# A three-layer transformer on one core: the norm in three slots, its modulation applied per channel after the transposition

## What is computed

```python
mod = silu(c) @ w_adaln + b_adaln                  # 6 vectors of 144 channels per sample
sh_msa, sc_msa, g_msa, sh_mlp, sc_mlp, g_mlp = split(mod, 6)
h = ln(x) * (1 + sc_msa) + sh_msa                  # ln: (x - mean) * rsqrt(var + eps), per token
x = x + g_msa * attention(h @ w_qkv + b_qkv) @ w_proj
h = ln(x) * (1 + sc_mlp) + sh_mlp
x = x + g_mlp * mlp(h)                             # layer 0: 4 experts, top 2; gelu
...
x = x + ((x @ U) @ expm(A(c)) - x @ U) @ U.T       # U = qr(P), after the three layers
```

## Time and profile before

| | us |
|---|---|
| median of 3 runs | 911.35 (909.35 to 921.39) |
| the profiled execution, its own time | 919.2 |
| its span, first to last instruction | 917.2 |
| TensorE matmuls busy in it | 751.5 |
| VectorE busy | 556.0 |
| ScalarE busy | 386.0 |
| GpSimd busy | 181.0 |
| mean granted TensorE clock (1.00 is full) | 0.856 |

### The profile page before, as it was taken

The page is one execution under the profiler, slowest core; times in us unless marked ns, Lnnn a source line. Parts: engine busy times, 40 slices in busy tenths (PEclk is TensorE's granted clock), DMA queues, the critical chain, the costliest instruction groups (busy, mean ns, idle before and its releaser), DMA issues.

```text
span 917.2 us, 11092 instructions
## 1 busy us (share of the span) xinstructions
PE 751.5 (82%) x3571; PEld 438.5 (48%) x3571; DVE 556.0 (61%) x1614; ACT 386.0 (42%) x690; POOL 181.0 (20%) x372
## 2 busy tenths in 40 slices
PE   6597889967998799798867886979897789979746
PEld 1353444335764445366444343645443555436325
DVE  3477787886327558752465777474787666785242
ACT  0221465534444544254235442435453356646511
POOL 5502012440132300302323003021003110021020
PEclk9955899989997669799977997976897988999957
DMA  3210100110121000012100000100000101000000
GB/s 88 69 35 7 32 14 22 39 31 13 48 56 32 1 24 13 12 33 60 39 18 1 24 12 13 32 1 1 24 13 11 33 1 25 12 12 1 13 1 13
DMA packets 22714, 21.23 MB, mean 23 GB/s; under 512 B 4831, under 2 KB 17015, under 8 KB 22658
## 3 DMA queue, kind: packets, MB, share of 16 engines
q1 hardware_dynamic: 22610, 20.52, 8.6%
q10 hardware_dynamic: 48, 0.02, 0.0%
HBM read 13.62 MB, written 0.61 MB: 16 GB/s over the span
## 4 chain that ended last, share of the span: by engine, by line
PE 62%; DVE 28%; issue 4%; ACT 2%; POOL 2%; DMA 0%; DVEq 0%; SPq 0%; ACTq 0%; POOLq 0%
PE m_bank L1400 11%; PE o_bank L1422 10%; DVE row_max L972 9%; PE s_bank L1383 8%; PE d_bank L1539 7%; PE d_bank L1483 3%; PE m_bank L1592 3%; PE m_bank L1409 2%; DVE h_tok L1031 2%; PE d_bank L1528 2%; PE d_bank L1440 2%; PE d_bank L1439 1%; PE d_bank L1454 1%; PE d_bank L1530 1%; PE d_bank L1529 1%
## 5 line engine op out<-in xcount | busy, mean ns | idle before, releaser
L797 ACT ACTIVATE probs<-s_bank 128x512 f32<-128x512 f32 x384 | 223.1, 598 | 380.4 <-PE s_bank L1383 377.1
L972 DVE TENSOR_REDUCE row_max<-m_bank 128x1 fp32r<-128x512 f32 x384 | 255.3, 686 | 91.8 <-PE m_bank L1400 86.5
L1400 PE MATMUL m_bank<-k_pad,q_t 128*128 128x512 f32 x348 | 173.1, 511 | 43.0 <-DVE row_max L972 12.6
L1383 PE MATMUL s_bank<-q_t,k_pad 128*128 128x512 f32 x384 | 176.3, 466 | 2.9 <-ACT probs L797 2.0
L1400 PEld LDWEIGHTS m_bank<-k_pad,q_t 128*128 128x128 f32 x348 | 72.1, 212 | 115.0 <-issue 36.8
L1422 PE MATMUL o_bank<-probs,v_aug 128*32 128x512 f32 x768 | 120.6, 704 | 0.7 <-ACT probs L797 0.7
L1383 PEld LDWEIGHTS s_bank<-q_t,k_pad 128*128 128x128 f32 x384 | 81.8, 215 | 30.1 <-ACT probs L797 15.4
L1539 PE MATMUL d_bank<-w,g_act 128*128 128x144 f32 (+1 forms) x480 | 61.8, 288 | 8.7 <-issue 8.7
L1539 PEld LDWEIGHTS d_bank<-w,g_act 128*128 128x128 f32 (+1 forms) x480 | 59.5, 190 | 14.2 <-issue 8.3
L714 POOL TENSOR_TENSOR h_tok<-h_tok,mod 128x144 f32<-128x144 f32 x48 | 23.7, 494 | 202.7 <-DVE h_tok L1031 202.7
L1592 PE MATMUL m_bank<-gram_rows,ident 64*64 64x208 f32 (+42 forms) x128 | 40.3, 403 | 16.0 <-DVE gram_rows L1207 15.6
(11 more groups left out here) (232 smaller groups left out, 1145.1 us busy)
## 6 DMA issues: line engine op xcount, KB each, us to landing
k_pad<-k_t SPq DMA_DIRECT2D x96, 64.0 KB, 2.0
raw_a<-in_L_cond_w_dram SPq DMA_DIRECT2D x10, 288.0 KB
w<-in_L_cond_w_dram SPq DMA_DIRECT2D x10, 288.0 KB
w_rows<-in_L_cond_W_dram SPq DMA_DIRECT2D x8, 141.8 KB
raw_d<-in_L_cond_w_dram SPq DMA_DIRECT2D x30, 36.0 KB
x_tok<-in_x_dram SPq DMA_DIRECT2D x2, 288.0 KB, 4.5
w<-in_L_cond_W_fc_dram SPq DMA_DIRECT2D x2, 288.0 KB
raw_a<-in_L_cond_W_fc_dram SPq DMA_DIRECT2D x2, 288.0 KB
```

What stands on the lines that cost most here:

```text
L797: act.activation(probs[:, n % PROBS, :], s_banks[n % S_BANKS][:, :], ACT.Exp, scale=HD ** -0.5)\
L972: dve.tensor_reduce(row_max[:, grp % 2, t, MAXROW + 32 * j:MAXROW + 32 * j + 1], bk[:, :], AX.X, ALU.max).then_inc(drained, 1)
L1383: pe.matmul(s_banks[n % S_BANKS][:, :], k_pad[:, grp % PADS, j, kt * P:(kt + 1) * P], q_t[:, par, g, :], start=True, stop=True).then_inc(s ...
L1400: ins = pe.matmul(bk[:, :], q_t[:, par, g, t * P:(t + 1) * P], k_pad[:, grp % PADS, j, :], start=True, stop=True)
```

## The change

- The norm of kinds "msa" and "mlp" has five slots, room 2, 1, 2, 1, 2: VectorE does the statistics in the first, the reciprocal root in the second, the scaling in the third, each with a fill ahead of it or in it; TensorE turns in the fourth and fifth; the hi, lo and d parts are made in the fifth. Kinds "o" and "x" become a stage `lay` of three slots, room 2, 1, 2.
- The modulation is no longer applied to tokens. `mods(l)` computes shift and 1 + scale per channel on partitions (`mod_a`, `mod_d`) by matmuls of two columns; `gates(l)` computes the two gates as before, for tokens. After the transposition ScalarE writes `h_hi` and `h_d` with scale and bias; VectorE computes `h_part` (rows 32 to 64) and `h_full`, and `h_lo` from `h_full` and `h_hi`; GpSimd subtracts for rows 32 to 64 of `h_d`.
- GpSimd only copies the last 16 channels. `x_tok` and `o_tok` rows are as wide as those of `h_tok`, so "o" and "x" are turned where they lie.
- Slots: `mods(0)` alone stands in HEAD, `gates(0)` in block 0, `mods(1)` and `mods(2)` in blocks 1 and 3, `gates(1)` in 2, `gates(2)` in 4. `load_ada(1)` leaves the start of SyncE's queue. GpSimd has a dozen more small constants.

```diff
-HEAD = [("mods", 0, 0), ("mods", 0, 1), ("prep", 0), ("norm", 0, "msa"), ("qkv", 0)]
+HEAD = [("mods", 0), ("prep", 0), ("norm", 0, "msa"), ("qkv", 0)]
...
-ROOM = {"prep": (), "mods": (1,), "norm": (4, 1, 2), ...
+ROOM = {"prep": (), "mods": (1,), "gates": (1,), "norm": (2, 1, 2, 1, 2), "lay": (2, 1, 2), ...
...
# GpSimd, norm
-                    if kind in ("msa", "mlp"):
-                        link(pool.tensor_tensor(tile, tile, mv[:, first + 1, :], ALU.mult))
-                        link(pool.tensor_tensor(tile, tile, mv[:, first, :], ALU.add))
-                    elif kind == "o":
-                        link(pool.tensor_copy(tile, o_tok[:, blk % 2, t, :]))
...
+                    pool.wait_ge(s["h_part_ready"], seen.next("modulated"))
+                    pool.wait_ge(s["h_d_ready"], seen.n["norm"])
+                    pool.tensor_tensor(h_d[32:64, :], h_part[32:64, :], h_d[32:64, :].bitcast(F32), ALU.subtract)\
+                        .then_inc(d_free, 1)
...
# ScalarE, norm, last slot
+                act.activation(h_hi[:, :], a_bank[:, :], ACT.Identity, scale=scale, bias=shift)\
+                    .then_inc(s["h_hi_ready"], 1)
+                act.wait_ge(s["h_part_ready"], seen.next("modulated"))
+                act.activation(h_d[:, :], d_bank[0:DW, :], ACT.Identity, scale=mod_d[:, l % 2, v + 1, b:b + 1],
+                               bias=mod_d[:, l % 2, v, b:b + 1]).then_inc(s["h_d_ready"], 1)
...
# VectorE, norm
+                    yield
+                    fill[0]()
                     link(dve.tensor_scalar(nwt[:, 1, 0:T], mean_var[:, :, 1], EPS, None, ALU.add))
                     rsqrt(rstd[:, :], nwt[:, 1, 0:T], nwt[:, 0, 0:T])
+                    yield
+                    fill[0]()
...
+                    dve.tensor_scalar(h_part[32:64, :], d_bank[32:64, :], mod_d[32:64, l % 2, v + 1, b:b + 1],
+                                      mod_d[32:64, l % 2, v, b:b + 1], ALU.mult, ALU.add)\
+                        .then_inc(s["h_part_ready"], 1)
+                    dve.wait_ge(s["h_hi_ready"], seen.n["norm"])
+                    link(dve.tensor_scalar(h_full[:, :], a_bank[:, :], mod_a[:, l % 2, v + 1, b:b + 1],
+                                           mod_a[:, l % 2, v, b:b + 1], ALU.mult, ALU.add))
+                    dve.tensor_tensor(h_lo[:, :], h_full[:, :], h_hi[:, :].bitcast(F32), ALU.subtract)\
+                        .then_inc(a_free, 1)
...
# TensorE, mods
+                for i, v in enumerate((0, 1, 3, 4)):
+                    for ada, c, first in ((ada_a, c_wide_a, True), (ada_d, c_wide_d, False)):
+                        pe.matmul(bk[:, B * i:B * (i + 1)], ada[:, v * C:v * C + P], c[:, :, 0], start=first,
+                                  stop=not first)
+                    for ada, c, first in ((ada_a, c_wide_a, True), (ada_d, c_wide_d, False)):
+                        for r in range(0, DW, 32):
+                            ins = pe.matmul(bk[r:r + 32, B * (4 + i):B * (5 + i)], ada[:, v * C + P:v * C + P + 32],
+                                            c[:, :, 0], start=first, stop=not first, skip_group_check=True)
```

More of the change, by code:

```diff
@@ L88, in stages @@
     if block == 0:
-        out += [("norm", 1, "msa"), ("qkv", 1), ("prep", 1), ("prep", 2), ("mods", 1, 0), ("prep", 3)]
+        out += [("norm", 1, "msa"), ("qkv", 1), ("gates", 0), ("prep", 1), ("prep", 2), ("prep", 3)]
     if block >= 1:
@@ L279, in load_order @@
     todo += [(mlp_at_step(m - 2) + 1 if m >= 2 else -1, ("w2", m)) for m in range(1, MLPS)]
-    todo += [(LAST_SLOT[("mods", 1, 1)], ("ada", 2))]
+    todo += [(LAST_SLOT[("gates", l - 1)], ("ada", l)) for l in range(1, LAYERS)]
     todo += [(-0.5, ("pad", grp)) for grp in range(PADS)]
@@ L343, in build @@
         h_d = sb("h_d", [DW, N], F32R)
+        h_part = sb("h_part", [DW, N])
+        h_full = sb("h_full", [P, N])
         ada_a = sb("ada_a", [P, 6 * C])
@@ L580, in _ @@
             load_w(1)
-            load_ada(1)
             load_item(1)
@@ L720, in norm @@
-                yield
-                ring.take(), ring.take()
-                yield
+                for t in range(T):
+                    if kind == "x":
+                        pool.wait_ge(s["x_done"], blk % B * 2 + t // 2 + 1)
+                    elif kind != "o":
+                        pool.wait_ge(s["xn_ready"], seen.next("xn_ready"))
+                    tile = token_tile(blk, kind, t)
+                    pool.tensor_copy(tile[:, P + 32:P + DW].rearrange("p (r w) -> p r w", r=2)[:, :, 0:CR],
+                                     tile[:, P:C].unsqueeze(1).to_broadcast([P, 2, CR]))\
+                        .then_inc(s["h_tok_ready"], 1)
+                    pool.wait_ge(s["h_tok_ready"], seen.next("h_tok_ready"))
@@ L802, in o_copy, with mods @@
                 act.activation(o_t[:, :], o_bank[:, :], ACT.Copy).then_inc(s["o_copied"], 1)
-            def norm(blk, kind):
+            mods_done = {}
+            def mods(l):
+                _, drained, before = ring.take()
+                mods_done[l] = (drained, before + 1)
+                yield
+            def norm(blk, kind):
+                b, l = blk % B, blk // B
+                v = 0 if kind == "msa" else 2
+                if kind in ("msa", "mlp"):
+                    yield
+                    yield
                 yield
@@ L1444, in norm @@
             def norm(blk, kind):
+                if not h_ready:
+                    pe.wait_ge(s["ident_ready"], 1)
+                if kind in ("msa", "mlp"):
+                    yield
+                    yield
                 yield
@@ L1644, in solver @@
                 last[chain] = ready
-            walk = {"mods": mods, "norm": norm, "qkv": qkv, "proj": proj, "gate": gate, "mlp": mlp,
-                    "rotate": rotate}
+            walk = {"mods": mods, "gates": gates, "norm": norm, "lay": norm, "qkv": qkv, "proj": proj, "gate": gate,
+                    "mlp": mlp, "rotate": rotate}
             def side(todo):
```

229 lines of the change are left out of this document (135 added, 94 removed).

## The result

The changed kernel took 955.53 us in the median of four runs (948.87 to 960.12), against 914.28 for the kernel before beside it (909.35 to 921.39). The ratio is 1.044, with a 95% interval of 1.034 to 1.054: it is slower, where I had said 877 us and a range that ended at 914. The profiled execution took 948.87 us. Some executions of either kernel are disturbed, at a lower clock and some per cent longer: a ratio leaves them out, a median holds them.

The account below looks back on a forecast made before the run. It took the kernel to be bound by TensorE and VectorE waiting for each other, chiefly at the norms, neither being full. Its terms summed to -34.3 us, from 911.35 to 877 us, with an 8-in-10 range of 849 to 914.

Parts of the forecast that it names:

- (h): Small things: earlier turning of "o" in blocks 1 and 2, loss 2 us; SyncE's loads and the rest hidden.
- (d): Clock behind the ten norms between steps: less time at half speed, gain 16 us, ends 0 and 32.
- Rival 2: Closings between steps: ScalarE held by VectorE, exponentials late, TensorE stands; slower, 944 us; chance 0.06.
- (a): HEAD's modulation: two-column matmul passes replace sixteen passes of 432 columns, gain 4.8 us.
- Rival 4: Modulation matmuls in HEAD and between steps: loads of 32 columns nearly free, 0.03 us each; 869 us; chance 0.11.
- (b): HEAD's norm: GpSimd's multiplication and addition go, transpositions end sooner, closing loses 0.9; gain 1.1 us in all.
- (c): Stalls at the ten norms between steps: VectorE's work in three parts frees TensorE, gain 20 us, ends 0 and 34.
- rival 1: Norms between steps: the stall only changes its place and the clock falls as before; 913 us; chance 0.22.
- (e): Modulation between steps: four groups go, three `gates` and two `mods` come; loss 2.1 us.
- (f): Closings between steps: `h_full` and the hold by GpSimd's subtraction, at most 19 us; loss 8 us put on the path.
- (g): TAIL: norm's transpositions end sooner, "o" and "x" need fewer copies; gain 4.5 us (2 to 6).

Follow-up runs that it names:

- e7: e1 with GpSimd's new constants set behind its old ones, away from VectorE's copies; 921.28 us, ratio 0.999 to the kernel before.
- e4: The kernel before with the msa and mlp norms divided in three VectorE slots, all else as before; 924.95 us, ratio 1.010.
- e1: The changed kernel with layer 0's gates behind the preparations of items 1 and 2, so their loads fall due earlier; 916.52 us, ratio 0.988.
- e8: e1 with the modulation behind the turn left out, so norms close as the plain ones do; 909.35 us, ratio 0.987.
- e10: e1 unchanged, run again in five rounds; 922.15 us, ratio 0.996 to the kernel before.
- e6: e1 with statistics and inverse root left out in all norms but the first; 892.24 us, ratio 0.969.

## Why the prediction was wrong, point by point

The step that failed is the last sentence of (h): "SyncE: without the wait for HEAD's modulation item 1 arrives sooner, and the later loads have half a block; hidden". I had moved the stages by their slots and had not asked what else is computed from those places. The loads' due times are, and the prep that moved has no slot of its own. Items 2 and 3 had not half a block but 0.06 us. Price: a wait of 25 to 27 us, shown by three runs; no rival of mine had it. The second step that failed is (d), 16 us for the clock, of which nothing came. Rival 2, the slower side, hardly occurred: ScalarE's wait for `h_part` came to 13.1 us in nine times, 2.1 at the longest, but TensorE's wait for the exponentials only rose from 2.0 to 4.7 us. (I had given it three score banks; the kernel has two.) That the result is slower is not that rival come true.

- *(a) HEAD's modulation*, 4.8 said. From 9.58 it ran for 5.76 us, where 13.9 stood: 8.2, less 1.1 for its later start. The passes of 128 columns took 0.26 us in HEAD, those of 32 took 0.21 / 6 = 0.035; I had 0.06 for the fast rate. Rival 4 had the price right. The mechanism was right, the size too small. The later start is that of the copies which e7 shortens. The Trainium skill, "TensorE: Matmul & The Clock Gate" (LDWEIGHTS (loading the stationary operand)), has the columns divided by 1.2 GHz, 0.027 for such a pass (an estimate); the trace has 0.028 between steps (0.17 / 6) and 0.035 in HEAD.
- *(b) HEAD's norm*, 1.1 said. The first linear matmul stood at 35.53 and is at 28.39: (a) and (b) gave 7.1 together where I had 5.9. The closing cost more than said, the transpositions less.
- *(c) The stalls*, 20 said: 8 us at the norms, 5 of them returned behind. Over all 384 steps, from HEAD's end to TAIL's start, the windows say more. Before, e4, e1 and e8:

```profile
73.58:866.11 792.53, 671.75 (x3311) 392.82 (x3310) 503.84 (x1457) 363.56 (x645) 146.89 (x297) 0.87 0.08 21
```
```profile
73.60:865.59 791.99, 680.75 (x3312) 394.44 (x3311) 501.57 (x1457) 362.80 (x645) 147.04 (x297) 0.86 0.08 21
```
```profile
66.46:862.08 795.62, 677.33 (x3432) 399.09 (x3431) 506.66 (x1461) 365.08 (x645) 121.97 (x207) 0.87 0.08 21
```
```profile
64.97:859.91 794.94, 695.28 (x3432) 407.01 (x3431) 497.57 (x1451) 362.65 (x645) 104.55 (x197) 0.85 0.08 21
```

Idle is 120.8 us before, 111.2 in e4, 118.3 in e1 (112.2 in e10) and 99.7 in e8, which has the divided norm, the old closing and none of GpSimd's work on tokens but the copies: 21 us less than before. So as idle time the gain of (c) came, half of it in e4 and all of it in e8, and the new closings took 12 to 19 of it back; this speaks against rival 1's "only changes its place". Yet none of these stretches is shorter by as much as 1 us: what left the idle time stands in the busy time. The step that failed is that idle time won is time won. Whether the busy time is its price, by the clock, or a draw is not shown: e1 and e10 differ by 20 us in it.
- *(d) The clock*, 16 said: nothing. The time at the lower level is the same within the draws, 115 and 127 us. The clock did not follow the length of the stall; without any statistics (e6) it hardly rose. In this half rival 1, with 0.22, was right.
- *(e) Modulation between steps*, a loss of 2.1 said. One `mods` took 3.85 us (297.66 to 301.5) where I had 4.6. Right within what can be seen.
- *(f) The closings*, 8 said: 14 to 21 us of idle time for twelve, 1 to 8 us of the run by the ratios. As idle time mis-sized, with every duration too low and the hold in the wrong place: `h_lo` took 0.69, not longer. It was the small operation behind it that waited for GpSimd's subtraction to end, 1.02 us in place of 0.21.

```profile
26.33 0.69 DVE L1118 TENSOR_TENSOR h_lo<-h_full,h_hi 128x512 fp32r<-128x512 f32 x1
26.94 0.15 DVE L1277 RECIPROCAL s_small<-m_bank 64x1 f32<-64x1 f32 x1
27.12 1.02 DVE L1281 SCALAR_TENSOR_TENSOR s_small<-gram_rows,s_small,neg_after 64x1 f32<-64x1 f32 x1
```
```profile
26.43 1.71 POOL L746 TENSOR_TENSOR h_d<-h_part,h_d 32x512 fp32r<-32x512 f32 x1 [4.61 <-ACT h_d L858]
```

The 1.02 ends at 28.14, and so does GpSimd's 1.71. In five of the twelve closings a small operation of VectorE is held like this, for 0.66 to 1.03 us in all. `h_lo`, with two SBUF inputs, ran its 0.69 us in all twelve, but it had begun 0.10 us ahead of the subtraction each time, so no run shows it as the second to come. For the lock that the Trainium skill describes ("SBUF — State Buffer", Who interferes with whom), where whoever issues first has the pair, these agree with the earlier trace rows, and so do e7's copies. By the same rule it is GpSimd that would wait for `h_lo`, which overlaps its 1.71 by 0.59 us; my price without a wait was 1.25. That is not shown.

- *(g) TAIL*, 4.5 said: 51.1 us before, 47.4 in the changed kernel, 45.6 in e1, so 3.7 to 5.5. Right.
- *(h)* apart from the loads: the earlier "o" transposition cost 1.9 us in e1's first eight steps of block 1 (12.69 against 10.83), 1 said.

Summed again, by the ratios: 78 us lie between 877 and 955.5. The kernel before stood 3 us higher beside the changed one. With its loads in time the change is 4 to 11 us under the kernel before (e10, e1) where I had 34, so 23 to 30 are missing from the terms; with the others put in as measured, (c) and (d) together gave about 5 of their 36, an estimate. The changed kernel in turn is 45 to 53 us over e10 and e1: 27 are the wait, 12 are blocks 3 and 4 at a lower clock in the one pair of traces, and 6 to 14 stay open.

## What to carry over

Where an order of work is computed, an edit to the list moves everything that is computed from it: before moving a stage, recompute each queue's list and read it against the one before, loads first, and look for the wait that has no slack. An idle time behind a busy engine is worth about what the run without that engine's work gives, so make that run first. Idle time won is not yet time won: e8 idled 21 us less over the steps than the kernel before and took as long for them. And with a clock that comes in draws of one or two per cent, compare idle time and busy time apart, with more than one trace of each.

## What the runs showed of the hardware

- One and the same program took 909.4 to 932.1 us, with 745.7 and 771.4 us of busy TensorE in two traces. Two executions can agree closely for long and then part: the changed kernel and e1 agree to 0.3 us per eight steps in block 0, to 0.05 from step 8 of block 1 to step 32 of block 2, and then differ by up to 3.6.
- GpSimd's subtraction of 32 x 512 took 1.71 us (`h_part`, `h_d`), that of 32 x 576 1.40 (`raw_d`, `lay_d`). The first overlaps VectorE's `h_lo` by 0.59 us in all twelve closings; no run has it alone.
- A scale and a shift per partition cost ScalarE 0.78 us per 96 or 128 x 512 from PSUM where a plain copy took 0.59, and VectorE 0.80 to 0.81 where a subtraction took 0.68.
- VectorE's copies of 256 columns took 0.71 and 1.16 us beside GpSimd's memsets, and 0.33 and 0.35 without them (e7). VectorE's small operations on two SBUF tensors took 0.66 to 1.25 us where 0.15 to 0.21 is usual, and ended within 0.02 us of a GpSimd subtraction that had begun before them.
- In HEAD the granted clock reads 1.00 over 9.58 to 15.34, while the passes of 128 columns take 0.26 us there and 0.155 between steps.
